# Statistics of the second norm for the last two token groups: from VectorE's statistics instructions to ScalarE's accumulator

## The chip, the cores and the metric

The kernel runs on one core of one Trainium2 chip. Its five engines work side by side: TensorE (PE, matmul), VectorE (DVE), ScalarE (ACT), GpSimd (POOL), and SyncE (SP), which issues most transfers. Each engine works through its own instructions strictly in the written order and waits for the others by semaphores. The metric is the device time of one execution in microseconds (us); the kernel before takes 204.89 us, the median of 3 runs (204.83 to 205.24).

## The reference

Two blocks over 64 sequences of 64 tokens with 128 features, all in f32. The second block holds all that the change touches: the norm of the new `x`, its quantisation in blocks of 16, and the feed-forward part.

```python
def _layernorm(x, axis=-1, eps=1e-05):
    m = jnp.mean(x, axis=axis, keepdims=True)
    v = jnp.var(x, axis=axis, keepdims=True)
    return (x - m) / jnp.sqrt(v + eps)
...
        def fp4_linear(x, w):
            xq = fp4_quant_dequant(x)
            wq = fp4_quant_dequant(w)
            return jnp.einsum('bsk,nk->bsn', xq, wq)
        gate = fp4_linear(x, w_gate)
        y = fp4_linear(x, w_up)
        h = jax.nn.silu(gate) * y
        return fp4_linear(h, w_down)
    x = x + _L0_xattn_ref(ctx_2048, _layernorm(x, axis=-1), mask_BxS2_fk1, mask_BxS2_fk1, L0_xattn_W_src, L0_xattn_b_src, L0_xattn_W_tgt, L0_xattn_b_tgt, L0_xattn_W_out, L0_xattn_b_out)
    x = x + _L0_ffn_ref(_layernorm(x, axis=-1), L0_ffn_w_gate, L0_ffn_w_up, L0_ffn_w_down)
```

The inner width is 352, and `fp4_quant_dequant` scales each block of 16 values by its largest magnitude and rounds to eight levels.

## The kernel before

The 4096 tokens are 32 tiles of 128 tokens (one token for each partition), in 8 groups (0 to 7) of 4 tiles. The first part of the program runs attention group by group, in steps k = 0 to 8. The second part runs the feed-forward block tile by tile: tile m has a gate matmul and an up matmul on TensorE (`gate_up`, L1090 and L1093), a Silu on ScalarE (`silu`, L540) and a product on VectorE (`h_product`, L843). Two tiles make a unit u, for which VectorE finds the block maxima and their reciprocals (`h_max` L851, `h_reciprocal` L857), ScalarE scales those (`h_inverse` L620), GpSimd multiplies by them (`y_unit` L391), ScalarE takes magnitudes (`h_abs` L601), VectorE rounds in two steps (`h_round` L864, L869) and GpSimd multiplies the scale back (`hq_unit` L406). Seven tiles after its gate matmul a tile is transposed (`h_transpose` L1105, copied by ScalarE in `hT_evac`, L614) and multiplied by the down weights (`down` L1125).

The order of everything is written out by hand: each engine has a loop over m or u with `if m == ...` lines. There is no scheduler.

The input of tile m is the quantised second norm of its group. Its chain is: `x2_add` (DVE, the new x of the group) → `stats2` (DVE, L670 and L675: four statistics and four aggregating instructions) → `rstd2_of` (POOL, L269 to L272: variance plus epsilon, minus mean, power −0.5) → `xn2_of` (POOL, L282, four tiles) → `block_max` (DVE, L739) → `scales2_of` (POOL, L289, L291) → `block_reciprocal` (DVE, L745) → `y_of` (POOL, L309) → `y2_abs` (ACT, L524) → `s3_round` (DVE, L750 and L754) → `xq_of` (POOL, L316) → `xq_transpose` (PE, L1075) → `xqT_evac` (ACT, L608). Groups 6 and 7 (`NG - 2` and `NG - 1`) run this chain within the feed-forward tiles. TensorE transposes group 6 at tile m = 21 and group 7 at m = 25.

Two of TensorE's waits matter below: the gate matmul of tile m waits for the product of tile m − 2, and its up matmul waits for the Silu of tile m − 1.

Of the kernel before, what the change touches and what calls it, by code (L numbers as in the profile page):

```python
# [58 lines left out]
def xattn_ffn(nc, x, ctxT, mask_pairs, mask_rows, WsT, bkvq, WtT, WoT, bo, wg, wu, wd, out):  # L59
    with ExitStack() as ctx:  # L60
# [30 lines left out]
        nm1, ve1, rs1, nb1 = (sb(n, [P, NT]) for n in ("nm1", "ve1", "rs1", "nb1"))  # L91
        st2, mv2 = sb("st2", [P, NT, 6]), sb("mv2", [P, NT, 2])
        nm2, ve2, rs2 = (sb(n, [P, NT]) for n in ("nm2", "ve2", "rs2"))


        cT = [sb(f"cT{s}", [P, 2, GT]) for s in range(4)]
# [79 lines left out]
        cT_halves = ctxT.rearrange("(c p) t -> p c t", p=P)  # L176
        t_place = evacuations()
        pad_ok = sem("pad_ok")
        w_halves = (slice(0, WALL // 2), slice(WALL // 2, WALL))

        def tiles(g):
            return slice(g * TILES, (g + 1) * TILES)
# [67 lines left out]
        def _(pool):  # L250
# [16 lines left out]
            def rstd2_of(g):  # L267
                pool.wait_ge(aggr2, g + 1)
                nc.gpsimd.tensor_scalar(ve2[:, tiles(g)], mv2[:, tiles(g), 1], EPS, 1.0, ALU.add, ALU.mult).then_inc(var2, 1)  # L269
                nc.gpsimd.tensor_scalar(nm2[:, tiles(g)], mv2[:, tiles(g), 0], -1.0, 0.0, ALU.mult, ALU.add).then_inc(nm2_ok, 1)  # L270
                pool.wait_ge(var2, g + 1)
                nc.gpsimd.tensor_tensor(rs2[:, tiles(g)], ve2[:, tiles(g)], minus_half[:, :], ALU.pow).then_inc(rstd2, 1)  # L272

# [106 lines left out]

            for k in range(NG + 1):
                attn_step(k)
            rstd2_of(NG - 2)
            xn2_of(NG - 2)

            def y_unit(u):
                i = u % 2
# [45 lines left out]
            for u in range(UNITS + 2):  # L433
                if 0 <= u - 2 < LAST_U:
                    hq_unit(u - 2)
                if u == 5:
                    xq_of(NG - 2)
                if u < UNITS:
                    h_scales(u)
                if u < LAST_U:  # L440
                    y_unit(u)
                if u == LAST_U:
                    y_tile(0)
                    y_tile(1)
                if u == UNITS + 1:
                    hq_first_tile()
                    residual_sum(D_BY_ACT[0])
                    residual_sum(D_BY_ACT[1])
                if u == 0:
                    xq_of(NG - 3)  # L450
                if u == 1:
                    scales2_of(NG - 2)
                if u == 2:
                    y_of(NG - 2)
                if u == 5:
                    rstd2_of(NG - 1)
                if u == 6:
                    xn2_of(NG - 1)
                if u == 7:
                    scales2_of(NG - 1)  # L460
                if u == 8:
                    y_of(NG - 1)
                if u == 10:
                    xq_of(NG - 1)

        @block.scalar
        def _(act):
# [160 lines left out]
            def down_evac(g):  # L628
                act.wait_ge(pe_dn, (g + 1) * TILES)
                past(act, out_d[g % 2], 16 * (g // 2))  # L630
                nc.scalar.copy(y_out[g % 2][:, :, :].rearrange("p t d -> p (t d)"), d_bank[:, :]).then_inc(d_ok, 1)

            for m in range(NT + LAG + 1):
                if m >= NT and (m - LAG - 1) % TILES == 0 and (m - LAG - 1) // TILES - 1 in D_BY_ACT:
                    down_evac((m - LAG - 1) // TILES - 1)
# [7 lines left out]
                    xqT_evac(m // TILES + 1)  # L643
                if m == 0:
                    y2_abs(NG - 3)
                if m == 8:
                    y2_abs(NG - 2)
                if m == 19:
                    y2_abs(NG - 1)
# [11 lines left out]
        def _(dve):  # L661
# [130 lines left out]
            def attn_step(k):  # L792
# [35 lines left out]
                    weights_round_down()  # L828
                if k == NG:
                    x2_add(NG - 2)  # L830
                    stats2(NG - 2)
                if on(g4) and g4 < NG - 3:
                    s3_round(g4)

# [74 lines left out]
            for m in range(NT + LAG + 2):  # L909
# [16 lines left out]
                    update(NG - 1)  # L926
                if m == 3:
                    x2_add(NG - 1)
                if m == 4:
                    block_max(NG - 2)  # L930
                if m == 6:
                    block_reciprocal(NG - 2)
                if m == 9:
                    s3_round(NG - 2)
                if m == 11:
                    stats2(NG - 1)
                if m == 15:
                    block_max(NG - 1)
                if m == 17:
# [297 lines left out]
```

## Time and profile before

| what | us |
|---|---|
| median of 3 runs | 204.89 (204.83 to 205.24) |
| the profiled execution | 205.46 |
| its span, first to last instruction | 203.2 |
| PE busy | 185.8 (91%) |
| DVE busy | 174.8 (86%) |
| POOL busy | 141.2 (70%) |
| ACT busy | 132.1 (65%) |

The span is divided into attention (to about 113 us) and feed-forward tiles (from there on). The busy shares are averages over both. The profiled execution takes 2.26 us more than its span. In the chain that ended last, PE has 50%, POOL 18%, DVE 8%, ACT 4%, and time in which an engine waited for nothing the profile shows ("issue") 12%. The granted TensorE clock is 9 tenths or more of full speed in all slices but the last.

### The profile page before, as it was taken

What the parts mean: (1) busy time and instruction counts of PE and PEld (TensorE: products, weight loads), DVE (VectorE), ACT (ScalarE), POOL (GpSimd) and SP (SyncE); (2) the same over time, 40 slices, a digit from 0 to 9 for tenths busy, and PEclk for the clock granted to TensorE, in tenths of its full rate; (3) what the DMA queues carried; (4) which work ended last, traced back from release to release, by engine and by line L of the source; (5) the groups of instructions that cost most, each with busy time, mean ns of one, the idle gap of its engine ahead of it and who ended that gap; (6) DMA issues with size and microseconds to landing.
All of it is one profiled execution on the core that took longest, in us unless ns stands there. A gap on an engine that the chain in (4) does not pass through costs nothing.

```text
span 203.2 us, 5834 instructions
## 1 busy us (share of the span) xinstructions
PE 185.8 (91%) x2105; PEld 142.6 (70%) x2105; DVE 174.8 (86%) x383; ACT 132.1 (65%) x280; POOL 141.2 (70%) x206
## 2 busy tenths in 40 slices
PE   5889989999889999999998999689999998999881
PEld 5564866859649788596785775467878676877780
DVE  6558989988998988969868888999999999999861
ACT  2066997959778699696868735485566564656740
POOL 6353691678898685954919577797999966868870
PEclk9999999999999999999999999999999999999997
DMA  5799970401200000000000000000101100110013
GB/s 199 236 239 345 353 250 7 155 5 31 75 3 2 3 3 5 0 0 3 5 3 0 3 2 0 0 5 0 53 0 55 43 9 0 55 50 5 0 59 99
DMA packets 13698, 11.99 MB, mean 59 GB/s; under 512 B 790, under 2 KB 10590, under 8 KB 13670
## 3 DMA queue, kind: packets, MB, share of 16 engines
q1 hardware_dynamic: 13086, 11.23, 18.0%
q10 hardware_dynamic: 584, 0.39, 0.6%
q8 instruction: 17, 0.28, 0.5%
q14 instruction: 11, 0.09, 0.2%
HBM read 9.52 MB, written 2.10 MB: 57 GB/s over the span
## 4 chain that ended last, share of the span: by engine, by line
PE 50%; POOL 18%; issue 12%; DVE 8%; DMA 4%; ACT 4%; SPq 1%; POOLq 0%; ACTq 0%; DVEq 0%
PE bank L1034 7%; PE bank L1125 5%; PE bank L1022 5%; POOL wq_y L391 5%; DMA x_all<-in_x 4%; POOL xn L282 3%; POOL hq L406 3%; PE bank L1093 3%; PE bank L1090 3%; PE bank L985 3%; PE bank L1105 3%; PE bank L1028 3%; PE bank L997 3%; PE bank L971 2%; PE bank L1043 2%
## 5 line engine op out<-in xcount | busy, mean ns | idle before, releaser
L1125 PE MATMUL bank<-wdT,hT 128*128 128x128 f32 x186 | 26.4, 278 | 1.8 <-issue 0.8
L1090 PE MATMUL bank<-guT,xqT 128*128 128x352 f32 x64 | 24.6, 465 | 2.2 <-DVE hh L843 2.2
L1125 PEld LDWEIGHTS bank<-wdT,hT 128*128 128x128 f32 x186 | 23.2, 191 | 3.1 <-issue 1.9
L1093 PE MATMUL bank<-guT,xqT 128*128 128x352 f32 x64 | 24.2, 460 | 0.0
L406 POOL TENSOR_TENSOR hq<-wq_u,sch 128x704 f32<-128x704 f32 x15 | 21.2, 1411 | 3.6 <-DVE wq_u L869 3.5
L391 POOL TENSOR_TENSOR wq_y<-hh,ivh 128x704 f32<-128x704 f32 x15 | 21.1, 1407 | 3.4 <-ACT ivh L620 2.8
L715 DVE TENSOR_REDUCE den<-prob 128x8 f32<-128x512 f32 x32 | 19.8, 667 | 0.0
L614 ACT COPY hT<-bank 128x384 f32<-128x384 f32 x32 | 15.2, 474 | 5.1 <-PE bank L1105 5.1
L1034 PE MATMUL bank<-wsT,cT 128*128 128x128 f32 x128 | 17.6, 281 | 0.8 <-DVE q_m L700 0.8
L843 DVE TENSOR_TENSOR hh<-bank,mask_bc 128x352 f32<-128x352 f32 x32 | 15.9, 496 | 1.6 <-PE bank L1093 1.2
L1034 PEld LDWEIGHTS bank<-wsT,cT 128*128 128x128 f32 x128 | 15.4, 191 | 2.5 <-DVE q_m L700 2.3
L1105 PE MATMUL bank<-ident,hq 128*128 128x128 f32 x96 | 15.8, 274 | 1.5 <-POOL hq L406 0.9
L1105 PEld LDWEIGHTS bank<-ident,hq 128*128 128x128 f32 x96 | 12.0, 141 | 7.4 <-issue 3.0
L1093 PEld LDWEIGHTS bank<-guT,xqT 128*128 128x128 f32 x64 | 12.0, 190 | 7.0 <-ACT mask_bc L540 0.6
L504 ACT ACTIVATE k_bd<-bank,bk_of,head_of 128x512 f32<-128x512 f32 x16 | 12.5, 786 | 6.3 <-PE bank L1022 6.3
L540 ACT ACTIVATE mask_bc<-bank 128x352 f32<-128x352 f32 x32 | 14.7, 458 | 2.9 <-PE bank L1090 2.6
L1022 PE MATMUL bank<-cT,wsT 128*128 128x512 f32 x32 | 15.4, 600 | 0.7 <-issue 0.7
L601 ACT ACTIVATE a_pair<-wq_y 128x704 f32<-128x704 f32 x15 | 11.5, 766 | 6.8 <-DVE wq_u L869 5.3
L851 DVE TENSOR_REDUCE amh<-hh 128x44 f32<-128x748 f32 x16 | 14.9, 929 | 0.4
L670 DVE BATCH_NORM_STATS2 st<-x_all 128x6 f32<-128x128 f32 x64 | 13.6, 276 | 1.7 <-DMA x_all<-in_x 1.4
L282 POOL TENSOR_SCALAR xn<-x_all,nm,rs 128x128 f32<-128x128 f32 x32 | 14.4, 462 | 0.8
L869 DVE SCALAR_TENSOR_TENSOR wq_u<-a_pair,mask_bc 128x704 f32<-128x704 f32 x15 | 13.4, 892 | 0.5
(136 smaller groups left out, 503.8 us busy)
## 6 DMA issues: line engine op xcount, KB each, us to landing
cT<-in_ctxT SPq DMA_DIRECT2D x8, 512.0 KB, 5.2
x_all<-in_x SPq DMA_DIRECT2D x8, 256.0 KB, 6.7
mask_bc<-in_mask_rows SPq DMA_DIRECT2D x8, 256.0 KB, 6.7
out_y<-mask_bc SPq DMA_DIRECT2D x7, 256.0 KB, 2.2
wsT<-in_WsT ACTq DMA_DIRECT2D x1, 256.0 KB, 5.0
out_y<-mask_bc SPq DMA_DIRECT2D x1, 192.0 KB, 2.0
w_all<-in_wg SPq DMA_DIRECT2D x1, 176.0 KB
w_all<-in_wu SPq DMA_DIRECT2D x1, 176.0 KB
```

What stands on the lines that cost most here:

```text
L282: last = nc.gpsimd.tensor_scalar(xn2[:, j * NB_X:(j + 1) * NB_X, :].rearrange("p n k -> p (n k)"), x_all[:, n, :], nm2[:, n:n + 1], rs2[:, ...
L391: nc.gpsimd.tensor_tensor(yh[i][:, :, :], hh[i][:, :, 0:BLK], ivh[i][:, :].unsqueeze(2).to_broadcast([P, 2 * NB_H, BLK]), ALU.mult).then_i ...
L406: nc.gpsimd.tensor_tensor(hq[i][:, :, 0:I].rearrange("p t (n k) -> p t n k", k=BLK), rh[i][:, :, :].rearrange("p (t n) k -> p t n k", t=2) ...
L614: nc.scalar.copy(hT[n % 2][:, :, :].rearrange("p c t -> p (c t)"), t_bank[place % 2][:, 0:IP]).then_inc(t_ok, 1)
L715: nc.vector.tensor_reduce(den[:, :, p, :], prob[g % 2][p][:, :, :].rearrange("r j (e s) -> r j e s", e=2), AX.X, ALU.add).then_inc(sum_ok, 1)
L843: nc.vector.tensor_tensor(hh[u % 2][:, t * NB_H:(t + 1) * NB_H, 0:BLK], gu_bank[(2 * n + 1) % 3][:, 0:I].rearrange("p (n k) -> p n k", k=BLK),
L1022: last = nc.tensor.matmul(w1[:, :], wsT[:, c, 0:D], cT[g % 4][:, c, :], start=(c == 0), stop=(c == 1))
L1034: last = nc.tensor.matmul(w0[:, j * P:(j + 1) * P], cT[g % 4][:, c, j * P:(j + 1) * P], wsT[:, c, D:2 * D], start=(c == 0), stop=(c == 1))
L1090: nc.tensor.matmul(gu_bank[2 * n % 3][:, 0:I], xqT[g % 2][:, t], guT[:, 0, :], start=True, stop=True).then_inc(pe_g, 1)
L1093: nc.tensor.matmul(gu_bank[(2 * n + 1) % 3][:, 0:I], xqT[g % 2][:, t], guT[:, 1, :], start=True, stop=True).then_inc(pe_u, 1)
L1105: last = nc.tensor.transpose(t_bank[place % 2][:, c * P:(c + 1) * P], hq[u % 2][:, n % 2, c * P:(c + 1) * P], ident[:, :])
L1125: last = nc.tensor.matmul(bank[:, j * P:(j + 1) * P], hT[n % 2][:, c, :], wdT[:, c, :], start=(c == 0), stop=(c == 2))
```

## The change

VectorE's statistics of groups 6 and 7 go. ScalarE makes them in the feed-forward tiles instead: for each tile of the group one pass over x with the identity function whose results are summed by the accumulator (`x2_sums`), then, once GpSimd has made minus the mean (`mean_of`), one pass that squares x minus mean, summed in the same way (`x2_squares`). From those sums GpSimd makes the variance and the power (`rstd_of_squares`). The full outputs of the passes go to `prob` buffers, which attention no longer uses. The later steps of group 6 move by two units or four tiles; those of group 7 keep their places.

```diff
@@ gpsimd
+            def mean_of(g):
+                pool.wait_ge(asum_ok, g - NG + 3)
+                nc.gpsimd.tensor_scalar(nm2[:, tiles(g)], sum2[:, tiles(g)], -1.0 / D, 0.0, ALU.mult, ALU.add).then_inc(nm2_ok, 1)
+
+            def rstd_of_squares(g):
+                pool.wait_ge(asq_ok, g - NG + 3)
+                nc.gpsimd.tensor_scalar(ve2[:, tiles(g)], ssq2[:, tiles(g)], 1.0 / D, EPS, ALU.mult, ALU.add).then_inc(var2, 1)
                 pool.wait_ge(var2, g + 1)
                 nc.gpsimd.tensor_tensor(rs2[:, tiles(g)], ve2[:, tiles(g)], minus_half[:, :], ALU.pow).then_inc(rstd2, 1)
...
             for k in range(NG + 1):
                 attn_step(k)
-            rstd2_of(NG - 2)
-            xn2_of(NG - 2)
...
-                if u == 5:
+                if u == 7:
                     xq_of(NG - 2)
...
+                if u == 0:
+                    mean_of(NG - 2)
+                if u == 2:
+                    rstd_of_squares(NG - 2)
+                    xn2_of(NG - 2)
+                if u == 3:
                     scales2_of(NG - 2)
-                if u == 2:
+                    mean_of(NG - 1)
+                if u == 4:
                     y_of(NG - 2)
                 if u == 5:
-                    rstd2_of(NG - 1)
+                    rstd_of_squares(NG - 1)
@@ scalar
+            def x2_sums(g, j):
+                act.wait_ge(x2_ok, g + 1)
+                for n in (g * TILES + j, g * TILES + j + 1):
+                    last = nc.scalar.activation(prob[0][g - NG + 2][:, n % TILES, :], x_all[:, n, :], ACT.Identity, accum_out=sum2[:, n:n + 1])
+                if j:
+                    last.then_inc(asum_ok, 1)
+
+            def x2_squares(g, j):
+                act.wait_ge(nm2_ok, g + 1)
+                for n in (g * TILES + j, g * TILES + j + 1):
+                    last = nc.scalar.activation(prob[0][g - NG + 4][:, n % TILES, :], x_all[:, n, :], ACT.Square, bias=nm2[:, n:n + 1],
+                                                accum_out=ssq2[:, n:n + 1])
+                if j:
+                    last.then_inc(asq_ok, 1)
...
-                if m == 8:
+                if m in (1, 2):
+                    x2_sums(NG - 2, 2 * (m - 1))
+                if m in (3, 4):
+                    x2_squares(NG - 2, 2 * (m - 3))
+                if m in (6, 7):
+                    x2_sums(NG - 1, 2 * (m - 6))
+                if m in (9, 10):
+                    x2_squares(NG - 1, 2 * (m - 9))
+                if m == 12:
                     y2_abs(NG - 2)
@@ vector
                 if k == NG:
                     x2_add(NG - 2)
-                    stats2(NG - 2)
...
-                if m == 4:
+                if m == 8:
                     block_max(NG - 2)
-                if m == 6:
+                if m == 10:
                     block_reciprocal(NG - 2)
-                if m == 9:
+                if m == 13:
                     s3_round(NG - 2)
-                if m == 11:
-                    stats2(NG - 1)
```

How the order of instructions reads on two engines follows; line numbers are those of each file.

ScalarE before, from the Silu of tile 9 to the Silu of tile 11 (`mask_bc` is where the Silu goes, `a_pair` the magnitudes of a unit, `hT` the copied transpose, `ivh` the scaled reciprocals):

```order
L540 ACTIVATE mask_bc<-bank 128x352
L608 COPY xqT<-bank 128x512
L614 COPY hT<-bank 128x384
L601 ACTIVATE a_pair<-wq_y 128x2x352
L540 ACTIVATE mask_bc<-bank 128x352
L620 ACTIVATE ivh<-ivr 128x44
L614 COPY hT<-bank 128x384
L540 ACTIVATE mask_bc<-bank 128x352
```

and the same place after the change:

```order
L556 ACTIVATE mask_bc<-bank 128x352
L624 COPY xqT<-bank 128x512
L659 ACTIVATE prob,ssq<-x_all,nm 128x128 x2
L630 COPY hT<-bank 128x384
L617 ACTIVATE a_pair<-wq_y 128x2x352
L556 ACTIVATE mask_bc<-bank 128x352
L636 ACTIVATE ivh<-ivr 128x44
L659 ACTIVATE prob,ssq<-x_all,nm 128x128 x2
L630 COPY hT<-bank 128x384
L556 ACTIVATE mask_bc<-bank 128x352
```

Group 7's squares now stand in tiles 9 and 10 ahead of a copied transpose, the magnitudes of unit 3 and the Silu of tile 10.

GpSimd before (with buffer numbers), from the product of unit 2 (`wq_y`) to the scaled result of unit 2 (`hq0` with `sch2`):

```order
L391 TENSOR_TENSOR wq_y<-hh0,ivh0 128x704
L309 TENSOR_TENSOR y2<-xn2,iv2 128x512
L406 TENSOR_TENSOR hq1<-wq_u,sch1 128x2x352
L398 TENSOR_SCALAR sch3<-amh1 128x44
L391 TENSOR_TENSOR wq_y<-hh1,ivh1 128x704
L406 TENSOR_TENSOR hq0<-wq_u,sch2 128x2x352
```

and after:

```order
L401 TENSOR_TENSOR wq_y<-hh0,ivh0 128x704
L282 TENSOR_SCALAR ve2<-ssq2 128x4
L284 TENSOR_TENSOR rs2<-ve2,minus_half 128x4
L294 TENSOR_SCALAR xn2<-x_all,nm2,rs2 128x128 x4
L416 TENSOR_TENSOR hq1<-wq_u,sch1 128x2x352
L408 TENSOR_SCALAR sch3<-amh1 128x44
L401 TENSOR_TENSOR wq_y<-hh1,ivh1 128x704
L301 TENSOR_SCALAR up2<-am2 128x32
L303 TENSOR_SCALAR sc2<-am2 128x32
L278 TENSOR_SCALAR nm2<-sum2 128x4
L416 TENSOR_TENSOR hq0<-wq_u,sch2 128x2x352
```

Variance, power and normalised x of group 6 came between attention and unit 0 before; now they stand between the product of unit 2 and the result of unit 1. Group 6's scales and group 7's minus mean stand behind the product of unit 3, ahead of the result of unit 2.

## Rows read from the trace of the kernel before

**Rows 1.** Busy time by stretch: us, then each engine's busy us (instructions), clock, DMA

```profile
130.00:140.00 10.00, 9.26 (x55) 7.05 (x56) 9.76 (x17) 6.46 (x15) 9.40 (x10) 1.00 0.01 2
140.00:150.00 10.00, 9.86 (x62) 7.72 (x61) 9.76 (x23) 6.00 (x14) 8.52 (x11) 1.00 0.09 27
150.00:160.00 10.00, 9.91 (x61) 7.70 (x60) 9.83 (x17) 5.32 (x13) 9.42 (x14) 1.00 0.09 28
160.00:170.00 10.00, 8.86 (x51) 6.44 (x49) 9.38 (x14) 5.79 (x14) 6.25 (x7) 1.00 0.09 26
```

**Rows 2.** Timeline of PE, gate matmuls: start, us, what, [idle before <-releaser]

```profile
128.37 0.83 PE L1090 MATMUL bank<-guT,xqT 128*128 128x352 f32 x2 [1.32 <-DVE hh L843]
...
138.33 0.76 PE L1090 MATMUL bank<-guT,xqT 128*128 128x352 f32 x2
...
140.52 0.76 PE L1090 MATMUL bank<-guT,xqT 128*128 128x352 f32 x2
...
170.70 0.76 PE L1090 MATMUL bank<-guT,xqT 128*128 128x352 f32 x2
...
173.21 0.76 PE L1090 MATMUL bank<-guT,xqT 128*128 128x352 f32 x2
...
175.83 0.76 PE L1090 MATMUL bank<-guT,xqT 128*128 128x352 f32 x2
```

**Rows 3.** Timeline of DVE, 110 to 172 us

```profile
115.53 0.38 DVE L675 BATCH_NORM_AGGREGATE mv<-st 128x2 f32<-128x6 f32 x4
...
117.00 0.69 DVE L750 SCALAR_TENSOR_TENSOR u<-a,y 128x512 f32<-128x512 f32 x1 [0.68 <-ACT a L524]
...
138.97 0.52 DVE L843 TENSOR_TENSOR hh<-bank,mask_bc 128x352 f32<-128x352 f32 x1
...
143.45 0.81 DVE L670 BATCH_NORM_STATS2 st<-x_all 128x6 f32<-128x128 f32 x4
144.29 0.38 DVE L675 BATCH_NORM_AGGREGATE mv<-st 128x2 f32<-128x6 f32 x4
...
165.61 1.76 DVE L754 SCALAR_TENSOR_TENSOR r<-a,u 128x512 f32<-128x512 f32 x1
...
169.15 0.46 DVE L843 TENSOR_TENSOR hh<-bank,mask_bc 128x352 f32<-128x352 f32 x1
```

**Rows 4.** Timeline of POOL, 110 to 172 us

```profile
122.71 1.06 POOL L316 TENSOR_TENSOR xq_all<-r,sc 128x512 f32<-128x512 f32 x1
...
127.88 0.32 POOL L289 TENSOR_SCALAR up<-am 128x32 f32<-128x32 f32 x1 [1.64 <-DVE am L739]
...
133.11 1.38 POOL L406 TENSOR_TENSOR hq<-wq_u,sch 128x704 f32<-128x704 f32 x1
...
136.36 1.39 POOL L406 TENSOR_TENSOR hq<-wq_u,sch 128x704 f32<-128x704 f32 x1
```

**Rows 5.** Timeline of ACT, 110 to 172 us

```profile
122.78 0.76 ACT L601 ACTIVATE a_pair<-wq_y 128x704 f32<-128x704 f32 x1 [0.43 <-POOL wq_y L391]
...
135.23 0.59 ACT L608 COPY xqT<-bank 128x512 f32<-128x512 f32 x1
135.70 0.50 ACT L614 COPY hT<-bank 128x384 f32<-128x384 f32 x1
...
137.13 0.45 ACT L540 ACTIVATE mask_bc<-bank 128x352 f32<-128x352 f32 x1
```

**Rows 6.** Groups over the whole span: busy us, mean ns, idle before and releaser

```profile
L282 POOL TENSOR_SCALAR xn<-x_all,nm,rs 128x128 f32<-128x128 f32 x32 | 14.4, 462 | 0.8
...
L474 ACT ACTIVATE xn<-x_all,nb,rs 128x128 f32<-128x128 f32 x28 | 11.5, 486 | 2.0 <-POOL nb L265 2.0
...
L272 POOL TENSOR_TENSOR rs<-ve,minus_half 128x4 f32<-128x4 f32 x8 | 8.1, 1017 | 0.0
...
L620 ACT ACTIVATE ivh<-ivr 128x44 f32<-128x44 f32 x16 | 3.9, 241 | 14.4 <-DVE ivr L857 14.4
```

**Rows 7.** The second rounding step of a group: count, ns min/median/max

```profile
L754 DVE SCALAR_TENSOR_TENSOR r<-a,u x8: 692/693/1759, 52.9 to 165.6; 128x512 f32<-128x512 f32 x8
```

More of the change, by code:

```diff
@@ L93, in xattn_ffn @@
         nm2, ve2, rs2 = (sb(n, [P, NT]) for n in ("nm2", "ve2", "rs2"))
+        sum2, ssq2 = sb("sum2", [P, NT]), sb("ssq2", [P, NT])
         cT = [sb(f"cT{s}", [P, 2, GT]) for s in range(4)]
@@ L178, in xattn_ffn @@
         pad_ok = sem("pad_ok")
+        asum_ok, asq_ok = sem("asum_ok"), sem("asq_ok")
         w_halves = (slice(0, WALL // 2), slice(WALL // 2, WALL))
@@ L270, in rstd2_of @@
                 nc.gpsimd.tensor_scalar(nm2[:, tiles(g)], mv2[:, tiles(g), 0], -1.0, 0.0, ALU.mult, ALU.add).then_inc(nm2_ok, 1)
+                pool.wait_ge(var2, g + 1)
+                nc.gpsimd.tensor_tensor(rs2[:, tiles(g)], ve2[:, tiles(g)], minus_half[:, :], ALU.pow).then_inc(rstd2, 1)
+            def mean_of(g):
[4 more added lines that the diff above has]
+                nc.gpsimd.tensor_scalar(ve2[:, tiles(g)], ssq2[:, tiles(g)], 1.0 / D, EPS, ALU.mult, ALU.add).then_inc(var2, 1)
                 pool.wait_ge(var2, g + 1)
@@ L450, in _ @@
                     xq_of(NG - 3)
-                if u == 1:
+                if u == 0:
[4 more added lines that the diff above has]
+                if u == 3:
                     scales2_of(NG - 2)
-                if u == 2:
+                    mean_of(NG - 1)
+                if u == 4:
                     y_of(NG - 2)
                 if u == 5:
-                    rstd2_of(NG - 1)
+                    rstd_of_squares(NG - 1)
                 if u == 6:
```

## Prediction, made before the changed kernel ran

> **What bounds the kernel now.** I read the busy time by stretch first, then each engine's timeline from 113 to 172 us, where all the changed instructions lie. In [rows 1] the reader sees three engines full at once: from 130 to 160 us VectorE is busy 9.8 of every 10 us, GpSimd 9.4, 8.5 and 9.4, TensorE 9.3 to 9.9, all at full clock. Only ScalarE has room (5.3 to 6.5). The gate matmuls [rows 2] show what TensorE needs: 138.33 to 140.52 is one tile without a stall, 2.19 us, and 173.21 to 175.83 one with a group's transpose, 2.62. From tile 12 (140.52) to tile 24 (170.70) it took 30.18 us; nine tiles at 2.19 and three at 2.62 are 27.6, so some 2.6 us of that stretch are stalls. From 173.21 on it runs without a stall nearly to the tail. The end is therefore set by when TensorE reaches tile 24, and until there it depends on VectorE's products and GpSimd's results.
>
> **Part 1: VectorE loses two sets of statistics.** One set is 0.81 + 0.38 us, 1.14 with its overlap (143.45 to 144.59) [rows 3]. Group 6's set ends at 115.9, and behind it VectorE stands idle 0.68 us until 117.00 for ScalarE's magnitudes of group 5 [rows 3], which this change doesn't hasten. That set is worth nothing. Group 7's set lies in the full stretch: up to −1.14 us.
>
> **Part 2: ScalarE gains 16 passes of 128x128.** No row of before has an accumulator. The nearest rows [rows 6]: 128x128 with two per-partition operands takes 486 ns and, back to back, 0.41 each (11.5/28); a short one of 44 columns takes 241. Below, a pair costs 0.5 us (a pass a little over the short one, overlapping). Above, 1.4 (each 0.48 plus a further small step of about 0.2 to read the sum out). I take 1.0, two passes near the 486 row, since the sum must be written too. That is 8 us of ScalarE's idle time in all, and by itself hidden: at tiles 1 and 2 the passes push the Silu of tile 3 back by some 0.2 us.
>
> The Trainium skill (ScalarE: Activation LUTs, "What ACT_TABLE_LOAD costs") gives 186 ns plus 0.833 a column for immediate operands, 93 more for each pointer operand, and 93 of overlap. It fits the 486 row (479). By it alone a pair of sums would be 0.5 us and a pair of squares 0.7, but it prices no accumulator. The same page's rules for kernel authors advise VectorE rather than ScalarE for adds and multiplies, thus against this change.
>
> **Part 3: the first new wait on ScalarE (tile 3).** The squares of group 6 wait for minus the mean, which GpSimd makes behind `xq_of` of group 5 (122.71 + 1.06 = 123.8 [rows 4]), so at about 124.05. ScalarE's queue is in order: behind the squares stand the magnitudes of unit 0, which started at 122.78 [rows 5] and would now start at 124.1 + 1.0 = 125.1, then the Silu of tile 4, which TensorE's up matmul of tile 5 needs. That matmul moves by about 2.2 us. But before, TensorE lost 1.32 us in front of tile 7 to VectorE's product [rows 2], and GpSimd 1.64 us waiting for group 6's block maximum [rows 4], which is now four tiles later. Most is paid from there: tile 7 starts about 0.6 us late (129.0 for 128.37), the result of unit 0 not at all.
>
> **Part 4: GpSimd's work moves out of its cover.** Group 6's variance, power and normalised x were done before unit 0, at 116 to 119.7, where nobody waited. They are 0.2 + 1.02 + 4 x 0.46 [rows 6], 3.1 us with gaps, now ahead of the result of unit 1; `y_of` of group 6 (1.0) leaves that place. Unit 1's result moves from 133.11 [rows 4] to about 135.2. Then `scales2_of` and group 7's minus mean (1.0 together) stand ahead of unit 2's result: 136.36 [rows 4] becomes 139.6.
>
> **Part 5: the second new wait on ScalarE (tile 9), which decides.** Group 7's squares wait for that minus mean, now made at about 139.55, behind the product of unit 3. ScalarE would be free for them at about 136. Behind them stand, in this order, a copied transpose (was 135.70), the magnitudes of unit 3, and the Silu of tile 10 (was 137.13) [rows 5]. After: 139.55 + 1.0 (squares) + 0.45 + 0.7 = 141.7, Silu of tile 10 done at 142.15. TensorE's up matmul of tile 11 (before 138.33 + 0.6 = 138.9 [rows 2]) can start at 142.35: 3.4 us late. The second pair of squares ahead of the next copied transpose adds 0.4: tile 12 at 144.35 for 140.52, **3.8 us late**.
>
> **Part 6: what is given back by tile 24.** TensorE alone could return 2.6 us, which leaves +1.2. VectorE: product of tile 10 about 142.2 for 138.97 (+3.2). From there to the product of tile 22 it took 30.18 us (138.97 to 169.15 [rows 3]). It now lacks the statistics (−1.14) and a wait of 0.44 and gains group 6's rounding and reciprocal, moved behind this point (+1.55): 30.15. In that stretch the second rounding step of group 7 took 1.76 us at 165.61 for a usual 0.69 [rows 3, 7]; if that doesn't recur, 29.1. So VectorE is 2.1 to 3.2 late at tile 22, and it had 1.1 us in hand (product of 22 ends at 169.6, gate of 24 at 170.70): +1.0 to +2.1. GpSimd would be some 3 to 4 us late from unit 4 to unit 9, without idle time; its idle time after 160 (6.25 busy of 10 [rows 1]) takes that back, and TensorE follows at +1.1 to +1.4. I take **+1.8 us**, in the upper part, since three engines with no room each seldom meet as tightly as each alone could. Behind tile 24 nothing of the change is left.
>
> **Sum:** 205.46 (profiled execution) + 1.8 = 207.3; on the median of the runs, 0.57 lower, 204.89 + 1.8 = **206.7 us**.
>
> **Rivals.**
> - *Nothing is given back.* The 3.8 us at tile 12 stay: 208.7. For it: [rows 1] has no engine of the three with room up to 160. Against: 2.6 us of TensorE's stalls there. 0.12.
> - *Rounding meets GpSimd.* VectorE's step with two SBUF inputs sometimes takes 1.07 us longer (692 to 1759 ns [rows 7]), at 165.61 beside a GpSimd multiply. Group 6's rounding moves from tile 9 to tile 13, beside GpSimd's result of unit 4. If both groups are hit, VectorE is 1.0 us later still: +2.8, 207.7. For it: GpSimd has no gaps there now. Against: it hit one of the last two groups before. 0.18. The Trainium skill (SBUF — State Buffer, "SBUF: two separate sides") has the two engines share one port pair as an exclusive lock for the whole instruction, which would make this the rule; the median of 693 ns says that it is mostly the other engine that waits.
> - *Wholly recovered*, within 0.2%: needs VectorE to save its 1.14 and the 1.07 and TensorE to run with no stall, and a pass near 0.25 us. 204.9. 0.06. Partly so (+0.4 to +0.9): 0.07.
> - *Faster: VectorE is the one bound.* From 140 to 160 it is full; taking 1.14 us out at 143.45 ends everything that much earlier: 203.8. It holds if ScalarE's wait at tile 9 is under about 1 us, so if GpSimd makes the mean by 137. Against: [rows 4] and part 4 put 3 us of new work ahead of that instruction. 0.06.
>
> The forecast itself (+0.9 to +2.4) has 0.51. A measurement of this kernel can tell 0.2% (0.4 us) from no change. Slower by more: 0.51 + 0.12 + 0.18 + 0.07 = 0.88. Same 0.06, faster 0.06. The range goes from 205.4 (+0.5) to 208.7 (+3.8): it leaves out faster, same, and some 0.07 at its two ends.
>
> **What would show it.** ScalarE idle before the squares: about 1.4 us at tile 3 and 3 us at tile 9, released by GpSimd's minus mean. Gate of tile 12 about 3.8 us late, of tile 24 1 to 2. GpSimd without idle time from unit 2 to 9. The passes at about 0.5 us. No change before 117 us. If ScalarE's wait at tile 9 is under 1 us, or if the gate of tile 12 is no later than 1.5 us, the forecast is wrong.

## The result and the profile after

| kernel | median us (lowest to highest, runs) | ratio to before, 95% interval |
|---|---|---|
| before | 204.86 (204.71 to 205.24, 4) | |
| after | 207.69 (207.40 to 208.36, 4) | 1.0133 (1.0114 to 1.0152) |

The change makes the kernel slower by 2.8 us. The forecast was +1.8 (206.7 us) with a range up to 208.7. The direction, the two new waits and their order came out as forecast. Two sizes did not, and they partly cancel. TensorE reaches tile 24 not 1.8 but 3.94 us late, and the tail of the program (what comes behind tile 31) returned some 1.3 us that the prediction did not look at.

The two new waits are in ScalarE's timeline of after (start, us, engine, line, operation, [idle before <-releaser]); lines "..." stand for the rows between the two places:

```profile
123.69 0.40 ACT L659 ACTIVATE prob<-x_all,nm 128x128 f32<-128x128 f32 x1 [1.61 <-POOL nm L278]
124.00 0.19 ACT L659 ACTIVATION_READ_ACCUMULATOR prob<-x_all,nm 128x1 f32 x1
124.09 0.39 ACT L659 ACTIVATE prob<-x_all,nm 128x128 f32<-128x128 f32 x1
124.38 0.19 ACT L659 ACTIVATION_READ_ACCUMULATOR prob<-x_all,nm 128x1 f32 x1
...
138.99 0.40 ACT L659 ACTIVATE prob<-x_all,nm 128x128 f32<-128x128 f32 x1 [3.81 <-POOL nm L278]
139.30 0.19 ACT L659 ACTIVATION_READ_ACCUMULATOR prob<-x_all,nm 128x1 f32 x1
139.39 0.39 ACT L659 ACTIVATE prob<-x_all,nm 128x128 f32<-128x128 f32 x1
139.68 0.19 ACT L659 ACTIVATION_READ_ACCUMULATOR prob<-x_all,nm 128x1 f32 x1
139.77 0.46 ACT L630 COPY hT<-bank 128x384 f32<-128x384 f32 x1
140.13 0.76 ACT L617 ACTIVATE a_pair<-wq_y 128x704 f32<-128x704 f32 x1
140.82 0.45 ACT L556 ACTIVATE mask_bc<-bank 128x352 f32<-128x352 f32 x1
```

The squares wait 1.61 us at tile 3 and 3.81 us at tile 9, both for GpSimd's minus mean. A pair of squares holds the queue 0.78 us (138.99 to 139.77), two passes and two short instructions that read the accumulator out. The Silu of tile 10 starts at 140.82 for 137.13 [rows 5].

Why the mean comes that late is in GpSimd's timeline of after, from behind the product of unit 2 to the result of unit 2:

```profile
131.45 0.19 POOL L282 TENSOR_SCALAR ve<-ssq 128x4 f32<-128x4 f32 x1
131.72 1.03 POOL L284 TENSOR_TENSOR rs<-ve,minus_half 128x4 f32<-128x4 f32 x1
132.86 1.73 POOL L294 TENSOR_SCALAR xn<-x_all,nm,rs 128x128 f32<-128x128 f32 x4
134.56 1.39 POOL L416 TENSOR_TENSOR hq<-wq_u,sch 128x704 f32<-128x704 f32 x1
...
138.76 0.20 POOL L278 TENSOR_SCALAR nm<-sum 128x4 f32<-128x4 f32 x1
138.91 1.38 POOL L416 TENSOR_TENSOR hq<-wq_u,sch 128x704 f32<-128x704 f32 x1
```

Unit 1's result comes at 134.56 (forecast 135.2, before 133.11), unit 2's at 138.91 (139.6, before 136.36 [rows 4]), the mean at 138.76 (139.55).

TensorE in after: its stalls, and the gate matmuls of tiles 12, 24 and 25 (141.05 is tile 11's), against [rows 2]:

```profile
125.65 0.86 PE L1129 MATMUL bank<-guT,xqT 128*128 128x352 f32 x2 [1.70 <-ACT mask_bc L556]
...
128.45 0.83 PE L1126 MATMUL bank<-guT,xqT 128*128 128x352 f32 x2 [0.32 <-DVE hh L881]
...
136.00 0.55 PE L1141 MATMUL bank<-ident,hq 128*128 128x128 f32 x3 [1.50 <-POOL hq L416]
...
140.28 0.94 PE L1161 MATMUL bank<-wdT,hT 128*128 128x128 f32 x6 [1.55 <-ACT hT L630]
141.05 0.76 PE L1126 MATMUL bank<-guT,xqT 128*128 128x352 f32 x2
...
143.35 0.76 PE L1126 MATMUL bank<-guT,xqT 128*128 128x352 f32 x2
...
174.64 0.76 PE L1126 MATMUL bank<-guT,xqT 128*128 128x352 f32 x2
...
177.15 0.76 PE L1126 MATMUL bank<-guT,xqT 128*128 128x352 f32 x2
```

Tile 7 starts at 128.45 for 128.37, so the wait at tile 3 has by then been paid from the stall that stood there (1.32 us in before, 0.32 now). Tile 12 starts at 143.35 for 140.52, +2.83. Tile 24 starts at 174.64 for 170.70, +3.94. Nothing is given back between them; another 1.1 us is lost. From tile 24 to tile 25 it is 2.51 us in both kernels.

Busy time by stretch in after, to be read against [rows 1]:

```profile
130.00:140.00 10.00, 7.23 (x41) 4.96 (x39) 8.04 (x13) 5.49 (x22) 9.30 (x14) 1.00 0.01 2
140.00:150.00 10.00, 9.72 (x57) 7.49 (x58) 8.53 (x15) 7.87 (x21) 7.90 (x10) 1.00 0.09 26
150.00:160.00 10.00, 9.06 (x55) 6.96 (x55) 9.83 (x16) 5.24 (x12) 9.50 (x13) 1.00 0.10 29
160.00:170.00 10.00, 9.15 (x57) 7.18 (x56) 8.94 (x15) 6.31 (x16) 8.41 (x9) 1.00 0.09 26
```

From 130 to 140 us TensorE falls from 9.26 to 7.23 and VectorE from 9.76 to 8.04, while GpSimd stays full (9.40 and 9.30): the engine that was given more work in this stretch is full, and the one that was relieved stands idle.

VectorE in after, from the product of tile 10 to that of tile 22, to be read against [rows 3]:

```profile
141.30 0.53 DVE L881 TENSOR_TENSOR hh<-bank,mask_bc 128x352 f32<-128x352 f32 x1 [3.06 <-ACT mask_bc L556]
...
149.96 1.42 DVE L789 SCALAR_TENSOR_TENSOR u<-a,y 128x512 f32<-128x512 f32 x1
151.42 0.69 DVE L793 SCALAR_TENSOR_TENSOR r<-a,u 128x512 f32<-128x512 f32 x1
...
166.67 0.53 DVE L881 TENSOR_TENSOR hh<-bank,mask_bc 128x352 f32<-128x352 f32 x1 [0.89 <-ACT mask_bc L556]
...
169.55 1.76 DVE L793 SCALAR_TENSOR_TENSOR r<-a,u 128x512 f32<-128x512 f32 x1
...
173.09 0.46 DVE L881 TENSOR_TENSOR hh<-bank,mask_bc 128x352 f32<-128x352 f32 x1
```

This stretch takes 31.79 us (141.30 to 173.09) for 30.18 before. The account closes: +1.55 for group 6's steps moved in, −1.14 for the statistics, +0.73 because the first of those steps takes 1.42 for a usual 0.69, +0.45 because the wait at tile 20's product is 0.89 for 0.44. That makes 31.77; the differences are read from rows of both traces, some of which are not shown here.

Last, the tail: VectorE's residual for the last tiles and SyncE's issue of the last two stores (SPq), before and then after.

```profile
197.88 0.56 DVE L882 TENSOR_TENSOR mask_bc<-bank,x_all 128x384 f32<-128x384 f32 x1 [1.94 <-PE bank L1125]
198.46 0.91 SPq L214 DMA_DIRECT2D out_y<-mask_bc  x2
198.71 0.29 DVE L882 TENSOR_TENSOR mask_bc<-a_pair,x_all 128x128 f32<-128x128 f32 x1 [0.28 <-PE a_pair L1125]
```

```profile
202.84 0.56 DVE L920 TENSOR_TENSOR mask_bc<-bank,x_all 128x384 f32<-128x384 f32 x1 [2.96 <-DMA out_y<-mask_bc]
203.32 0.28 DVE L920 TENSOR_TENSOR mask_bc<-a_pair,x_all 128x128 f32<-128x128 f32 x1
203.43 0.90 SPq L216 DMA_DIRECT2D out_y<-mask_bc  x2
```

And SyncE's waits in this tail (engine and line, what for: us in total, times, longest), before and then after:

```profile
SPq L247 <- DMA out_y<-mask_bc: 3.4, 1, 3.4
```

```profile
SPq L249 <- DMA out_y<-mask_bc: 1.3, 1, 1.3
```

In after the residual waits for an earlier store to leave its buffer, 2.96 us where before has 1.94 for TensorE's matmul, and ends at 203.60 for 199.00, +4.6. The last two stores are issued by 204.33 for 199.37, +5.0. But the wait for the last store is 1.3 us for 3.4. So the span grows by 2.8 (206.0 for 203.2), and that is also what the timed runs show.

### The profile page after: what moved, and what is told of

Same layout as the page of the kernel before. It is cut to its first block, busy times and chain, and to the rows that moved or that the text cites. A ratio compares the mean times of both kernels' runs of the same rounds, so it can differ in the third digit from the quotient of the medians.

```text
span 206.0 us, 5850 instructions
## 1 busy us (share of the span) xinstructions
PE 186.0 (90%) x2105; PEld 142.4 (69%) x2105; DVE 173.5 (84%) x367; ACT 136.9 (66%) x312; POOL 140.7 (68%) x206
## 4 chain that ended last, share of the span: by engine, by line
PE 44%; POOL 18%; issue 17%; DVE 12%; ACT 5%; DMA 2%; DVEq 0%; POOLq 0%; ACTq 0%
PE bank L1070 7%; POOL wq_y L401 5%; PE bank L1058 4%; PE bank L1161 4%; POOL xn L294 3%; POOL hq L416 3%; PE bank L1064 3%; PE bank L1021 3%; PE bank L1033 3%; PE bank L1126 2%; PE bank L1129 2%; PE bank L1007 2%; PE bank L1080 2%; PE bank L1079 2%; DVE u L789 2%
## 5 line engine op out<-in xcount | busy, mean ns | idle before, releaser
L294 POOL TENSOR_SCALAR xn<-x_all,nm,rs 128x128 f32<-128x128 f32 x32 | 13.9, 448 | 0.8
L902 DVE SCALAR_TENSOR_TENSOR mask_bc<-a_pair,wq_y 128x704 f32<-128x704 f32 x15 | 13.1, 875 | 0.0
```

Source lines behind the costliest of these rows:

```text
L294: last = nc.gpsimd.tensor_scalar(xn2[:, j * NB_X:(j + 1) * NB_X, :].rearrange("p n k -> p (n k)"), x_all[:, n, :], nm2[:, n:n + 1], rs2[:, ...
```

## The experiments

Theory: the loss is made on the way to tile 24, by GpSimd's moved steps and by ScalarE's two waits, and the removed statistics bring nothing. Rivals: the 16 passes themselves cost it; VectorE's late rounding (the steps held up by GpSimd) does; the relief of VectorE is real and hidden under the rest.

All runs side by side. The columns, each read from a profile: time from the gate matmul of tile 0 to that of tile 12, from there to tile 24, from tile 0 to tile 31, SyncE's wait for the last store, the span; then the median of all runs and the ratio to before on the same chip.

| kernel | 0 to 12 | 12 to 24 | 0 to 31 | last store | span | median | ratio (95%) |
|---|---|---|---|---|---|---|---|
| before | 27.11 | 30.18 | 73.33 | 3.4 | 203.2 | 204.86 | |
| after | 30.08 | 31.29 | 77.42 | 1.3 | 206.0 | 207.69 | 1.0133 (1.0114 to 1.0152) |
| mean7_early | 28.48 | 31.39 | 75.91 | 1.3 | 205.2 | 206.39 | 1.0106 (1.0074 to 1.0138) |
| passes_only | 26.96 | 30.22 | 73.22 | 1.3 | 201.5 | 204.17 | 1.0009 (0.9971 to 1.0047) |
| steps6_moved | 27.49 | 31.65 | 75.18 | 1.3 | 203.3 | 207.09 | 1.0129 (1.0064 to 1.0193) |
| group7_only | 27.12 | 30.09 | 73.25 | 1.2 | 201.0 | 203.76 | 0.9992 (0.9959 to 1.0025) |
| round7_next_tile | 27.11 | 29.25 | 73.34 | 2.9 | 202.6 | 204.94 | 0.9984 (0.9960 to 1.0008) |
| no_stats7 | 27.11 | 30.19 | 73.35 | 1.3 | 201.1 | 203.37 | 0.9925 (0.9896 to 0.9955) |
| both_means_early | 27.52 | 31.36 | 74.93 | 1.2 | 202.7 | 205.36 | 1.0019 (0.9993 to 1.0045) |
| group7_only_round | 27.11 | 29.10 | 73.20 | 1.2 | 201.5 | 203.23 | 0.9924 (0.9898 to 0.9951) |
| before_again | 27.11 | 30.18 | 73.33 | 3.2 | 203.0 | 204.88 | 0.9979 (0.9960 to 0.9998) |
| after_again | 30.08 | 31.30 | 77.42 | 1.3 | 207.3 | 207.89 | 1.0133 (1.0097 to 1.0170) |
| group7_round_again | 27.41 | 28.80 | 73.19 | 1.2 | 201.0 | 203.51 | 0.9913 (0.9884 to 0.9941) |

The kernel before beside them had a median of 203.92 us in the first four (24 runs, 203.08 to 206.44), 205.17 in the next four (24) and 205.26 in the last (17). The stretch from tile 0 to 31 agrees between two profiles of one kernel to 0.01 us in all three pairs, its split at tile 12 once only to 0.3 us (group7_only_round, 27.11 and 27.41). What comes behind tile 31 moved by 0.9 us between the two profiles of after, and the wait for the last store differs by 2 us between kernels. So causes are read from the tiles, and the ratio only says what is left of them. The ratio has a limit of its own: before_again, which is the kernel before against itself, came out at 0.9979 (0.9960 to 0.9998), so a ratio within some 0.4% of 1 shows nothing; the prediction took 0.2% as enough.

**mean7_early**, the change with group 7's minus mean one unit earlier:

```diff
                 if u == 2:
+                    mean_of(NG - 1)
                     rstd_of_squares(NG - 2)
                     xn2_of(NG - 2)
                 if u == 3:
                     scales2_of(NG - 2)
-                    mean_of(NG - 1)
```

> The kernel after, with group 7's minus mean one unit earlier in GpSimd's order (behind the product of unit 2, ahead of group 6's variance). Theory W (the wait for that mean at tile 9, 3.81 us in the profile after, is the main loss, and GpSimd's order makes it): ScalarE's wait before the squares of group 7 goes from 3.81 us to under 0.5, the gate matmul of tile 12 comes at about 141.7 us for 143.35, and the time is 206.2 us (205.9 to 206.6), 1.5 below the kernel after. Rival P (the 16 passes themselves load ScalarE): no less than 207.2. Rival O (the later place of group 6's steps on GpSimd costs it all): the wait is gone but GpSimd's result of unit 2 is as late as before, about 139 us, and the time stays within 0.4 us of 207.7.

Measured: ScalarE no longer waits at its squares of tile 9. Tile 12 comes 1.60 us sooner, and at tile 31 1.51 of it is left (75.91 for 77.42). So the late mean is worth 1.5 us and isn't given back. The time, 206.39 us, is in the expected range, but by the ratios (1.0106 for 1.0133) the timed gain is only some 0.6 us, with intervals that overlap; the 1.5 us is shown by the tiles alone. Tile 12 is still 1.37 late against before.

**passes_only**, the kernel before with the 16 passes added at the same places and nobody waiting for them (the squares take group 6's minus mean as bias; nothing uses the sums):

```diff
+                if m in (1, 2):
+                    x2_sums(NG - 2, 2 * (m - 1))
+                if m in (3, 4):
+                    x2_squares(NG - 2, 2 * (m - 3))
+                if m in (6, 7):
+                    x2_sums(NG - 1, 2 * (m - 6))
+                if m in (9, 10):
+                    x2_squares(NG - 1, 2 * (m - 9))
```

> The kernel before plus ScalarE's 16 passes at the tiles of the change; nobody waits for them, the squares of both groups take group 6's mean, which is long there, and their sums are not used; statistics stay on VectorE. Theory W: the passes are hidden, 204.9 to 205.3 us. Rival P: most of the 2.8 us of the change shows here, 206.5 or more.

Measured: 73.22 for 73.33, so the passes are free. This rival falls. What they take is in the trace's summary of the two lines (count, ns min/median/max), the squares first:

```profile
L642 ACT ACTIVATE prob<-x_all,nm x8: 387/398/422, 122.4 to 138.5; 128x128 f32<-128x128 f32 x8
L642 ACT ACTIVATION_READ_ACCUMULATOR prob<-x_all,nm x8: 187/197/212, 122.7 to 138.8; 128x1 f32 x8
```

```profile
L637 ACT ACTIVATE prob<-x_all x8: 293/296/312, 118.8 to 131.2; 128x128 f32<-128x128 f32 x8
L637 ACT ACTIVATION_READ_ACCUMULATOR prob<-x_all x8: 185/187/192, 119.0 to 131.4; 128x1 f32 x8
```

**steps6_moved**, the kernel before with only group 6's later steps moved as in the change; all statistics stay on VectorE:

```diff
-            rstd2_of(NG - 2)
-            xn2_of(NG - 2)
...
-                if u == 1:
-                    scales2_of(NG - 2)
                 if u == 2:
+                    rstd2_of(NG - 2)
+                    xn2_of(NG - 2)
+                if u == 3:
+                    scales2_of(NG - 2)
+                if u == 4:
                     y_of(NG - 2)
...
-                if m == 4:
+                if m == 8:
                     block_max(NG - 2)
```

(`block_reciprocal`, `s3_round`, `y2_abs` and `xq_of` move in the same way.)

> The kernel before with group 6's later steps at the places of the change (variance, power and normalised x in unit 2, scales in unit 3, product in unit 4, block maximum at tile 8, reciprocal at 10, magnitudes at 12, rounding at 13, result in unit 7); statistics stay on VectorE, no pass on ScalarE. Theory W: GpSimd's 3.1 us of work leave their cover, TensorE waits about 1.5 us for the result of unit 1 at tile 9, part comes back: 205.6 to 206.4 us. Rival O: 207.0 or more. If it stays at 204.9, the move costs nothing and the waits of ScalarE are all.

Measured: 75.18, so +1.85 us without any pass or wait of ScalarE. Only 0.38 of that is there at tile 12; the stretch to tile 24 loses 1.47. The place at which GpSimd's steps strike first is this one, TensorE's transpose of unit 1:

```profile
135.68 0.55 PE L1106 MATMUL bank<-ident,hq 128*128 128x128 f32 x3 [1.87 <-POOL hq L404]
```

Before, the stall at this transpose was 0.62 us. Most of the difference had been earned just ahead: tile 9 comes 1.0 us sooner than before (18.30 for 19.29 from tile 0). The tiles by themselves would make some 206.7 us, just above the 205.6 to 206.4 of theory W. The median of four runs, 207.09, lies where rival O was put (207.0 or more), and the ratio is as high as that of after, so by the timed runs alone the moved steps would be the whole loss. The profile is of the shortest of the four (205.53 of up to 207.66 us); what the others had more isn't in it, and after's tiles take 2.24 us more than these. I go by the tiles.

**group7_only**, the change for group 7 alone, its mean in unit 2, group 6 as before (shown against the changed kernel, in part):

```diff
+            rstd2_of(NG - 2)
+            xn2_of(NG - 2)
...
                 if u == 2:
+                    mean_of(NG - 1)
...
-                if m in (1, 2):
-                    x2_sums(NG - 2, 2 * (m - 1))
-                if m in (3, 4):
-                    x2_squares(NG - 2, 2 * (m - 3))
                 if m in (6, 7):
                     x2_sums(NG - 1, 2 * (m - 6))
```

> Only group 7's statistics on ScalarE, its minus mean behind group 6's product in unit 2; group 6 wholly as before. Theory W: no wait before the squares, GpSimd's order as before but for 0.25 us, VectorE 1.14 us shorter at tile 11: 203.9 to 204.7 us, faster than before if VectorE is a bound in 140 to 160 us. Rival P: the eight passes cost, 205.5 or more. Rival B (VectorE is not the bound there): 204.9 to 205.2.

Measured: 73.25 for 73.33, timed 0.9992. Taking group 7's statistics off a VectorE that is 9.8 of 10 us busy gains nothing, and done in this way costs nothing either.

**no_stats7**, the kernel before without group 7's statistics; its norm uses those of group 6, so that part of the computation is left out:

```diff
-                if m == 11:
-                    stats2(NG - 1)
```

> The kernel before without VectorE's statistics of group 7; that group's variance and mean are computed from group 6's statistics, so this part of the computation is left out. It prices the relief of VectorE alone. If VectorE is the bound from 140 to 160 us (the prediction's faster rival), gate 0 to gate 24 falls by 1.1 us from 57.29. Theory W after the run with group 7 alone on ScalarE (57.21): by 0.0 to 0.3 us, because the next long rounding and the wait for group 7's product of GpSimd come at the same time as before.

Measured: 73.35 for 73.33. This is the pure worth of the relief: none. Tile 20 is 0.38 us earlier (45.84 for 46.22), tile 24 not at all. Where the 1.14 us goes is in VectorE's timeline of this kernel:

```profile
162.56 0.53 DVE L844 TENSOR_TENSOR hh<-bank,mask_bc 128x352 f32<-128x352 f32 x1 [1.22 <-ACT mask_bc L541]
```

and in ScalarE's, just before:

```profile
160.49 0.63 ACT L525 ACTIVATE a<-y 128x512 f32<-128x512 f32 x1 [2.35 <-POOL y L310]
```

VectorE waits 1.22 us here for 0.44 in before (1.46 in all between products 10 and 22): for a Silu that stands in ScalarE's queue behind group 7's magnitudes, which wait for GpSimd's `y_of`. GpSimd is without a pause from 149 to 162 us in this kernel, so `y_of` comes no sooner, and a faster VectorE waits for it. The ratio of 0.9925 is not made in the tiles; it is the tail again (last store 1.3 us for 3.4).

**round7_next_tile**, the kernel before with group 7's rounding one tile later (`m == 20` → `m == 21`):

> The kernel before with group 7's two rounding steps one tile later on VectorE, behind the reciprocals of unit 10 (tile 21) and no longer ahead of the product of tile 21. Theory L (a GpSimd operation that has started holds VectorE's two-operand step up until it ends, and what stands behind pays): the second step moves away from the result of unit 8 but meets the product of unit 10, so it may still take up to 1.76 us; but the product of tile 21 and the reciprocals of unit 10 come 2.4 us earlier, TensorE loses its 0.5 us stall at tile 23, and gate 0 to gate 24 takes 56.5 to 56.9 us for 57.29: 204.1 to 204.6 on the scale where before is 204.9. Rival N (the long step is harmless): 57.2 to 57.4 and no difference in time.

Measured: the second step is long again (167.28, 1.75 us), beside another GpSimd multiply (167.06, 1.43). Tile 24 starts 0.93 us sooner, at 56.36 us from tile 0, even a little before the 56.5 to 56.9 of theory L, but tile 31 does not (73.34), and the time is that of before, as rival N had it. The 0.93 us is lost between tiles 24 and 25, at the first down matmul of a group:

```profile
171.54 0.68 DVE L876 TENSOR_TENSOR mask_bc<-bank,x_all 128x512 f32<-128x512 f32 x1
```

```profile
172.32 0.91 PE L1125 MATMUL bank<-wdT,hT 128*128 128x128 f32 x6 [0.96 <-issue]
```

By the program this matmul waits until VectorE's residual has read the bank (`yo_ok` in `down`). The rounding stands ahead of that residual in both places, VectorE has no less to do before it, and it ends 58.96 us after tile 0 for 58.95 in before. Group 7's own transpose, at 174.25, waits for nothing. So a held rounding step there costs nothing that could be had by moving it by one tile.

**both_means_early**, the change with both means ahead of what they stood behind:

```diff
                 if u == 0:
-                    xq_of(NG - 3)
-                if u == 0:
                     mean_of(NG - 2)
+                    xq_of(NG - 3)
                 if u == 2:
+                    mean_of(NG - 1)
                     rstd_of_squares(NG - 2)
                     xn2_of(NG - 2)
                 if u == 3:
                     scales2_of(NG - 2)
-                    mean_of(NG - 1)
```

> The kernel after with both minus means earlier in GpSimd's order: group 6's ahead of the result for group 5 in unit 0, group 7's in unit 2. ScalarE's wait at tile 3 falls from 1.61 to about 0.6 us and TensorE's stall there from 1.7 to about 0.7. Theory W: against the kernel with only group 7's mean earlier (gate 0 to gate 24 59.87 us) little is won, 59.3 to 59.9, because GpSimd's result of unit 1, held by group 6's chain, stands ahead of TensorE at tile 9 in either. Rival (the tile 3 wait is worth its length): 58.9 or less.

Measured: the wait at tile 3 falls from 1.61 to 0.59 us, and TensorE's stall behind it from 1.70 to this:

```profile
124.82 0.86 PE L1128 MATMUL bank<-guT,xqT 128*128 128x352 f32 x2 [0.68 <-ACT mask_bc L555]
```

Tile 24 comes 58.88 us after tile 0, which is the rival's side (58.9 or less) and not the 59.3 to 59.9 of theory W. Tile 31 comes 0.98 us sooner than in mean7_early (74.93 for 75.91), and at tile 12 only 0.41 is left to before. So the wait at tile 3 had a price of 1.0, about as much as was taken off it, which the gate of tile 7 alone did not show. What remains is the moved chain: 31.36 from tile 12 to 24, as in every kernel in which group 6's steps stand late (31.29 to 31.65), and 30.09 to 30.22 in those in which they don't and the rounding is in its place. Timed, this version is the kernel before within the interval, though its tiles take 1.6 us more; its last store waits 1.2 us for 3.4.

**group7_only_round**, group7_only with group 7's rounding at `m == 21`:

> Group 7's statistics alone on ScalarE (its mean in unit 2, group 6 as before) and group 7's rounding one tile later. With nothing of group 6 moved, and the rounding out of the way of tile 21's product, the 1.14 us taken from VectorE can show: gate 0 to gate 24 at 56.0 to 56.7 us for 57.29, 0.4 to 1.0 us faster than before. If the rounding was harmless: 57.2 as with group 7 alone.

Measured: 203.23 us, ratio 0.9924, the fastest that was run. Tile 24 comes at 56.21 as expected, but the tiles to 31 take 73.20 for 73.33. The gain of 1.5 us is nearly all in the last store (1.2 for 3.4). Three repeats were to show whether such differences stay: **before_again** and **after_again** are the two kernels unchanged, **group7_round_again** this one.

> The kernel before itself, word for word, as a control on the same chip and in the same hour as the three kernels beside it. Ratio 1.000 within 0.2%. Its profile should show gate 0 to gate 31 at 73.3 us again; what differs from the first profile (203.2 us of span) is the head and the wait for the last store (3.4 us there, 1.3 in most of the other profiles).

> The kernel after, word for word. Gate 0 to gate 31 at 77.4 us as in its first profile (73.3 before). If the first comparison (+2.8 us) was cut short by the first profile's long wait for the last store in the kernel before, the difference here is up to 4.7 us where before has the short wait, and 2.6 to 3 us where it has the long one.

> Group 7 alone on ScalarE and its rounding one tile later, word for word as before. Its profile showed gate 0 to gate 31 at 73.20 us for 73.33, so by the feed-forward tiles it should be 0 to 0.2 us faster than before; its first comparison gave 0.9924 (1.5 us). If that was the last store's wait, the ratio here depends on what before does: 0.998 to 1.000 where before has the short wait, 0.992 where it has the long one.

Measured: before_again has its long last wait again (3.2 us) and a ratio of 0.9979, whose interval ends just short of 1; after_again has the same +4.09 in the tiles and the short wait; group7_round_again is at 0.9913. The order of the three holds. What does not hold is the reference: in the first four comparisons the kernel before had 203.92 us and group7_only tied with it, in the others 205.2. I read the advantage of 1.5 us as one over a tail that the kernel before mostly, but not always, has.

**chain6_behind**, both_means_early with group 6's variance, power and normalised x behind the result of unit 1, and its steps on VectorE and ScalarE one tile later:

```diff
+                if u == 3:
+                    rstd_of_squares(NG - 2)
+                    xn2_of(NG - 2)
...
-                if m == 13:
+                if m == 14:
                     s3_round(NG - 2)
```

> Both minus means early, and group 6's variance, power and normalised x behind GpSimd's result of unit 1 instead of ahead of it; its block maximum, reciprocal, magnitudes and rounding one tile later. TensorE's stall of 1.82 us for that result at tile 9 goes. Theory W (it is GpSimd's 3.1 us of added work in the full stretch, wherever it stands): the stall comes back at the result of unit 2 by tile 11, and gate 0 to gate 31 takes 74.5 to 75.3 us for 74.93 with both means early. Rival (the place ahead of that result is what costs): 73.3 to 74.2, and the time of before.

Measured: 207.05 to 208.24 us in five runs, ratio 1.0105 (1.0074 to 1.0137), slower than both_means_early. Its profiled execution was another thing altogether, 373.69 us, with these gate matmuls (busy us, mean ns):

```profile
L1126 PE MATMUL bank<-guT,xqT 128*128 128x352 f32 x64 | 47.4, 839 | 0.0
```

for a mean of 465 ns in after. No times of the tiles can be taken from it, so why this order is worse stays open, and how much of it is the tail. The fastest of its five runs is 2.2 us above the fastest of both_means_early, where the rival wanted 0.7 to 1.6 us less. That speaks against the hope that GpSimd's chain only has to leave unit 1's way; it doesn't settle it.

## Why the prediction came out as it did

| cause, between tiles 0 and 31 | us | from |
|---|---|---|
| 16 passes | −0.1 | passes_only less before |
| group 6's moved steps, with passes and hardly a wait | +1.6 | both_means_early less before |
| wait for group 6's mean (tile 3) | +1.0 | mean7_early less both_means_early |
| wait for group 7's mean (tile 9) | +1.5 | after less mean7_early |
| sum | +4.1 | after less before |

The first row is within the second, so it isn't added again. The last three are steps along one chain of kernels, so their sum is closed by construction, and in another order a row could come out otherwise: steps6_moved, with no pass and no wait of ScalarE, has +1.85 where the second row has +1.6. What within the moved steps costs it (GpSimd's three microseconds ahead of unit 1, group 6's rounding beside a GpSimd multiply, or `y_of`) was not taken apart by a run; group 6's rounding was never moved alone.

*Part 1, right.* Group 6's set is worth nothing: VectorE stands idle for ScalarE's magnitudes 1.61 us in its place, and goes on at 116.86 for 117.00 (after starts its tiles 0.14 earlier). Group 7's set is worth nothing either (no_stats7), where the part allowed up to −1.14.

*Part 2, right in its kind, the size too high.* Hidden, as forecast. A pair takes 0.59 us for sums and 0.78 for squares, not 1.0; both bounds hold (0.5 and 1.4). The step that reads the sum out exists as a separate instruction of 0.19 us, but it overlaps with the next pass, so that squares come every 0.39 us. By the formula of the Trainium skill (ScalarE: Activation LUTs, "What ACT_TABLE_LOAD costs") a pair is estimated at 0.5 and 0.7; the trace lies nearer to it than to my value, with about 0.1 more a pair, for what it doesn't price.

*Part 3, right in place.* TensorE's up matmul of tile 5 waits 1.70 us (2.2 forecast), tile 7 is 0.1 to 0.2 late in place of 0.6. But "most is paid from there" was wrong as an account. That stall and GpSimd's idle time were not for this wait alone; with the moved steps they could be spent once, and both_means_early shows 1.0 us of price.

*Part 4, right in time, wrong in weight.* Unit 1's and unit 2's results move as forecast to within 0.7 us. By itself that costs 0.4 us at tile 12 (steps6_moved).

*Part 5, right in mechanism, the size too high.* Measured 2.97 from tile 0 to 12 (30.08 for 27.11) for 3.8. The mean is made 0.8 us sooner than forecast (138.76), and the squares take 0.2 less than 1.0.

*Part 6, wrong; this is the step that failed.* Of 3.8 us, 2.0 were to be given back by tile 24; of the real 2.97 nothing was, and 1.11 came on top. The term behind it was VectorE's stretch from product 10 to product 22, put at 30.15 or 29.1 us and measured at 31.79. Three things in it: the wait of 0.44 did not go but doubled (0.9 us of error), since ScalarE waits longer for GpSimd's `y_of` (2.40 us for 1.96); group 6's first rounding step was held by GpSimd for 0.73; and group 7's second step was again 1.76, where one case hoped for 0.69. The rival *rounding meets GpSimd* thus happened on both groups. It was given 0.18 because the median of all eight rounding steps was 693 ns; but five of these eight stand in the attention part and say little of a stretch in which GpSimd has no gap. The row also leaves out the first steps, one of which took 2.13 us in before (50.71 to 52.84, beside a GpSimd multiply of 2.59). (That rival's time, 207.7, is the measured one; in part by accident, as the last paragraph of this section shows.) I also took TensorE's 2.6 us of stalls between 12 and 24 as a reserve. They are not one: where TensorE waits for a chain that comes later itself, the wait stays. Nor does the end hang on tile 24 alone, as the prediction's first paragraph has it: in round7_next_tile tile 24 came 0.93 us sooner and tile 31 did not.

Why the timed +2.8 is nearer to +1.8 than the tiles' +4.1: VectorE's last residual comes 4.7 us late counted from tile 0 and the last store waits 2.1 us less. So the forecast's number was helped by something that it did not hold. This is luck: +4.1 by itself would have lain beyond the +3.8 at which the range ended. The runs of the kernel before beside the first four experiments had a median of 203.92 us, and from there to the 207.69 of after it is 3.8 us; these two were not timed beside each other, so this is a hint only.

## What to carry to other kernels

An engine at 98% is not the limit just because it is full: taking 1.14 us out of it gained 0.0 here, for GpSimd's in-order queue set the pace behind it. Before a step is offloaded, ask at which place in the helper's queue the handshake will stand; two instructions of 0.2 us, one a single place and the other one unit too late, cost 1.0 and 1.5 us, and the sixteen passes that they fed cost nothing. Don't count another engine's stalls as a reserve if what ends them is late as well.

## What the runs showed of the hardware that was not expected

*VectorE's steps with two inputs in SBUF and GpSimd's multiplies exclude each other, and it can be timed.* A step of VectorE that began while a GpSimd multiply was running ended 0.54 to 0.55 us after that multiply, in eight cases in six kernels (two in before, two in after, one each in mean7_early, steps6_moved, both_means_early and round7_next_tile). In round7_next_tile, VectorE and then GpSimd:

```profile
167.28 1.75 DVE L754 SCALAR_TENSOR_TENSOR r<-a,u 128x512 f32<-128x512 f32 x1
```

```profile
167.06 1.43 POOL L391 TENSOR_TENSOR wq_y<-hh,ivh 128x704 f32<-128x704 f32 x1 [0.31 <-ACT ivh L620]
```

GpSimd ends at 168.49, VectorE at 169.03. In steps6_moved the step that began later in the multiply (148.57, with GpSimd's from 147.53 to 148.92) was held for less, 0.90 us in all, and ended at 149.47. After has 149.45 + 1.38 = 150.83 and 149.96 + 1.42 = 151.38. GpSimd is held in turn; in after its next two instructions, beside the end of VectorE's first step and beside the second, are long:

```profile
150.92 0.69 POOL L408 TENSOR_SCALAR sch<-amh 128x44 f32<-128x44 f32 x1
151.69 1.67 POOL L401 TENSOR_TENSOR wq_y<-hh,ivh 128x704 f32<-128x704 f32 x1
```

for a usual 0.36 and 1.39. By this the trace agrees with the Trainium skill (SBUF — State Buffer, "SBUF: two separate sides"), which has one lock for the whole instruction. The price for VectorE's step, 0.69 us if it is free, is what was left of the multiply less some 0.15: 0.73 of 0.87 in after, 1.06 of 1.21 in round7_next_tile.

*The last store.* SyncE waits 2.9 to 3.4 us for it in before, before_again and round7_next_tile, and 1.2 to 1.3 in each of the ten other profiles that can be used, though the code of the tail is the same. That is more than the effect of most edits here. A store can also be late one place earlier: VectorE's residual for the last tiles waits for TensorE in nine of the thirteen profiles (1.94 to 1.96 us), but for an earlier store in steps6_moved (2.11), mean7_early (2.60), after (2.96) and after_again (3.79). None of these four has the long last wait. What decides it wasn't found.

*One execution in chain6_behind* ran its matmuls at about half the rate (839 ns for 465) with the granted clock shown at full (1.00, the level of 2.4 GHz), while VectorE's products took 525 ns for 498 in after. The cause isn't known.
